# A four-layer graph network on one core: third norm merged with the attention projections, comparisons ahead of the scan, and an earlier clearing of a buffer

## The reference, cut to what matters

```python
x = _layernorm(x + _L0_gnn_ref(x, src, dst, edge_weight, W1, W2))     # two weighted sums over edges
x = _layernorm(x + _L1_gnn_ref(x, weight, w_comp, root, bias, ...))   # eight edge types
x = _layernorm(x + _L2_gnn_ref(x, W, b, src, dst, edge_weight))       # logmap, sum, relu, expmap
x = _layernorm(x + _L3_gnn_ref(x, edge_index, W, att_src, att_dst, bias))

# _L3_gnn_ref: attention with 8 heads of 16
xp = (x @ W).reshape(N, H, C)
a_src = einsum('nhc,hc->nh', xp, att_src);  a_dst = einsum('nhc,hc->nh', xp, att_dst)
e = leaky_relu(a_src[src] + a_dst[dst], 0.2)
m = segment_max(e, dst);  ex = exp(e - m[dst])
alpha = ex / (segment_sum(ex, dst)[dst] + 1e-16)
out = segment_sum(xp[src] * alpha[:, :, None], dst) + bias
```

## Time and profile before

| | us |
|---|---|
| median of 3 runs (lowest to highest) | 9468.76 (9463.22 to 9489.17) |
| profiled execution, its own time | 9472.64 |
| span of that execution | 9470.8 |

### The profile page before, as it was taken

The page is one execution under the profiler, slowest core; times in us unless marked ns, Lnnn a source line. Parts: engine busy times, 40 slices in busy tenths (PEclk is TensorE's granted clock), DMA queues, the critical chain, the costliest instruction groups (busy, mean ns, idle before and its releaser), DMA issues. The chain is left out here.

```text
span 9470.8 us, 285464 instructions
## 1 busy us (share of the span) xinstructions
PE 7599.4 (80%) x87223; PEld 6468.6 (68%) x87223; DVE 6462.5 (68%) x21922; ACT 2902.1 (31%) x8008; POOL 5787.9 (61%) x5766
## 2 busy tenths in 40 slices
PE   4887999998999996899999957999945666666662
PEld 4886999996999995466666646787834555555552
DVE  7997777775777776677777766676764555555556
ACT  3884222223222224322222242122241222222222
POOL 2663777773777772166666624666625777777771
PEclk7998999999999997999999978999976566655665
DMA  2002666664666665633333335555532222222223
GB/s 63 28 27 72 157 161 154 155 158 135 153 154 151 152 155 168 220 92 87 90 87 88 88 103 146 135 142 139 140 104 74 65 66 66 66 66 67 67 66 102
DMA packets 1057653, 1044.16 MB, mean 110 GB/s; under 512 B 171994, under 2 KB 957065, under 8 KB 1056897
## 3 DMA queue, kind: packets, MB, share of 16 engines
q1 hardware_dynamic: 869802, 654.88, 24.9%
q0 software_dynamic: 174080, 369.69, 16.8%
q10 hardware_dynamic: 13399, 16.26, 0.5%
HBM read 877.56 MB, written 169.10 MB: 111 GB/s over the span
## 5 line engine op out<-in xcount | busy, mean ns | idle before, releaser
L1048 DVE TENSOR_SCALAR state<-iota_row,state 128x128 f32<-128x128 f32 x5488 | 1444.4, 374 | 0.0
L1561 POOL DMA_INDIRECT state<-rel_table,state x1120 | 1065.2, 951 | 504.9 <-issue 323.1
L1107 PE MATMUL psum<-ring 128*128 128x128 bf16 x21276 | 1275.5, 221 | 58.1 <-DVE ring L1041 58.1
L1107 PEld LDWEIGHTS psum<-ring 128*128 128x128 bf16 x21276 | 1208.2, 99 | 109.8 <-issue 42.5
L1027 POOL DMA_INDIRECT ring<-rows,idx x980 | 957.5, 977 | 368.6 <-issue 327.7
L1027 POOL DMA_INDIRECT ring<-gcn_table,idx x980 | 957.5, 977 | 352.6 <-issue 324.8
L2612 POOL DMA_INDIRECT acc<-att_table,acc x896 | 935.0, 1043 | 273.1 <-issue 263.6
L1276 POOL DMA_INDIRECT state<-hyp_table,state x784 | 751.4, 958 | 419.5 <-issue 217.8
L2612 POOL DMA_INDIRECT ring<-att_table,acc x672 | 698.0, 1039 | 441.4 <-ACT acc L2654 245.4
L1122 PE MATMUL psum<-state 64*128 64x128 f32 x14112 | 958.7, 278 | 0.0
L1041 DVE TENSOR_SCALAR ring<-sel,iota_col 128x640 bf16<-128x640 bf16 (+1 forms) x1576 | 513.4, 369 | 600.3 <-PE psum L1107 581.6
(11 more groups left out here) (444 smaller groups left out, 14711.7 us busy)
## 6 DMA issues: line engine op xcount, KB each, us to landing
ring<-xparts SPq DMA_DIRECT2D x1332, 192.0 KB
ring<-srow SPq DMA_DIRECT2D x544, 128.0 KB
sel<-drow SPq DMA_DIRECT2D x394, 160.0 KB
sel<-drow SPq DMA_DIRECT2D x394, 128.0 KB
rel_table<-tout SPq DMA_DIRECT2D x98, 512.0 KB, 2.6
ring<-rows SPq DMA_DIRECT2D x56, 448.0 KB
xparts<-state SPq DMA_DIRECT2D x28, 672.0 KB, 3.6
rows<-acc SPq DMA_DIRECT2D x42, 448.0 KB
```

What stands on the lines that cost most here:

```text
L1048: ins = nc.vector.tensor_scalar(picks[u][:, j, :], iota_row[:, :], tabS[:, bass.ds(n * SJ + j, 1)], tabW[:, bass.ds(n * SJ + j, 1)], ALU.i ...
L1107: last = nc.tensor.matmul(rowsP[v][:, j * P:(j + 1) * P], reach[v][:, t, j * P:(j + 1) * P], xwin[u][:, t, i, :], start=(t + i == 0), stop ...
L1561: pool.indirect_dma_start(out=type_rows[j % RB][:, k, :], out_offset=None, in_=table, in_offset=bass.IndirectOffsetOnAxis(ap=type_idx[j % ...
```

## The change

- The third norm and the attention projections become one block, norm_into_attention. ACT scales the tiles into a stage instead of in place; the rows are stored and transposed from there. The transposes of even and odd blocks use two pairs of banks (0 and 1, 2 and 3). Each engine runs its steps with a lag to the others: DVE scales block b+2, copies the transposed rows of block b+1, adds and takes statistics of block b+3, and copies the product of block b.
- In the attention pass the selection is made by eight TENSOR_SCALAR comparisons of 128x128 instead of one TENSOR_TENSOR of 128x1024, and comes ahead of the scan; DVE waits for the scan's own end before it goes on.
- The row no_sums lies in rown and is filled in the setup; body is cleared in the sort, one DMA of 256 rows with each piece and one for the rest, and no longer in the first cell pass. An unused table, starts8, goes.

```diff
-        no_sums = sq[:, 0:ROW7]
+        no_sums = rown[:, 0:2, :].rearrange("p a t -> p (a t)")[:, 0:ROW7]
...
+                c(nc.vector.memset(no_sums[:, 0:ME], 0.0))
+                c(nc.vector.memset(no_sums[:, ME:ROW7], -BIG))
...
+                    def clear_rows(j):
+                        at = j * (PT * P)
+                        sp.dma_start(body[bass.ds(at, PT * P), :].rearrange("(t p) c -> p t c", p=P),
+                                     no_sums.unsqueeze(1).to_broadcast([P, PT, ROW7])
+                                     ).then_inc(sem("kept1"), 16)
...
                             keep(it * 2 + v)
                             load(it * 2 + (v + 2), v)
+                            clear_rows(it * 2 + v)
...
-                        if table is rows0:
-                            sp.dma_start(body[bass.ds(sg * SUMS, SUMS), :].rearrange("(t p) c -> p t c", p=P),
-                                         no_sums.unsqueeze(1).to_broadcast([P, SUMS // P, ROW7])
-                                         ).then_inc(sem("kept1"), 16)
...
+        def norm_into_attention():
...
+                @block.sync
+                    def step(it, u):
+                        load(it, u)
+                        keep(it, u)
+                        keep_table(it, u)
...
+                @block.scalar
+                            act.wait_ge(sem("var"), b + 1)
+                            nc.scalar.activation(sd[:, v, :], mv[:, v, :, 1], ACT.Sqrt, bias=eps_t[:, :]
+                                                 ).then_inc(sem("sdev"), 1)
+                            act.wait_ge(sem("scaled"), b + 1)
+                            act.wait_ge(sem("rowsT"), b + 1)
+                            act.wait_ge(sem(f"kept{v}"), turn * 16 + 16)
+                            act.sem_inc(sem("issued"), 1)
+                            for t in range(BT):
+                                last = nc.scalar.activation(stage[:, v, t * P:(t + 1) * P],
+                                                            acc[:, bass.ds(b * BW + t * P, P)], ACT.Identity,
+                                                            bias=shift[:, v, t:t + 1], scale=rstd[:, v, t:t + 1])
...
+                @block.tensor
+                    def transpose_block(it, u):
+                        b, v, _ = block_at(it, u, 2)
+                            pe.wait_ge(sem("normed"), b + 3)
+                            pe.wait_ge(sem("xTfree"), b + 1)
+                            for t in range(BT):
+                                last = nc.tensor.transpose(pblk(v)[:, t * P:(t + 1) * P],
+                                                           stage[:, v, t * P:(t + 1) * P], ident[:, :])
...
+                    def product(it, u):
+                        b, v, _ = block_at(it, u, 1)
+                            pe.wait_ge(sem("xTready"), b + 1)
+                            pe.wait_ge(sem("tB"), b + 1)
...
+                @block.vector
+                    def step(it, u):
+                        normalise(it, u)
+                        columns(it, u)
+                        sums_and_spread(it, u)
+                        table_rows(it, u)
...
                             nc.vector.tensor_tensor_scan(runmax, starts_T[w], sT, -BIG, ALU.add, ALU.max
                                                          ).then_inc(sem("runmax"), 1)
+                            dve.wait_ge(sem("runmax"), n + 1)
...
-                            nc.vector.tensor_tensor(
-                                sel_of[w], iota_row[:, :].unsqueeze(1).to_broadcast([P, K, P]),
-                                dstrel[:, bass.ds(n * K, K)].unsqueeze(2).to_broadcast([P, K, P]),
-                                ALU.is_equal).then_inc(sem("selected"), 1)
+                            for k in range(K):
+                                ins = nc.vector.tensor_scalar(sel_of[w][:, k, :], iota_row[:, :],
+                                                              dstrel[:, bass.ds(n * K + k, 1)], None,
+                                                              ALU.is_equal)
+                            ins.then_inc(sem("selected"), 1)
...
+                        select(i)
                         scan(i)
-                        select(i)
...
-                residual_norm("hyp", rows2, rows3 if layers > 3 else out)
+            if layers > 3:
+                norm_into_attention()
...
-            project("att")
             attention()
```

More of the change, by code:

```diff
@@ L698, in _ @@
                             load(it * 2 + (v + 2), v)
+                            clear_rows(it * 2 + v)
                     keep(PIECES - 3)
+                    for j in range(PIECES // 2 * 2 - 2, PIECES):
+                        clear_rows(j)
+                    sp.dma_start(body[PIECES * PT * P:NPAD, :].rearrange("(t p) c -> p t c", p=P),
+                                 no_sums.unsqueeze(1).to_broadcast([P, NPAD // P - PIECES * PT, ROW7])
+                                 ).then_inc(sem("kept1"), 16)
                     load(PIECES - 1, 0)
@@ L1010, in _ @@
                                 load(sg * GB + it * 4 + u, it * 4 + u, u)
-                    if table is rows0:
-                        sp.wait_ge(sem("kept1"), (SG + 1) * 16)
                     for u in range(4):
@@ L1051, in to_sources @@
                         ins.then_inc(sem("picked"), 1)
-                    if table is rows0:
-                        nc.vector.memset(no_sums[:, ME:ROW7], -BIG)
-                        nc.vector.memset(no_sums[:, 0:ME], 0.0).then_inc(sem("made"), 1)
                     nc.vector.memset(zeros_b, 0.0).then_inc(sem("sent"), 1)
@@ L2326, in project, with lagged, block_at, is_block @@
             fence()
+        def lagged(eng, step, lead):
+            for b in range(-lead, 0):
+                step(0, b)
+            with eng.Fori(0, NB // 2 - 3) as it:
+                step(it, 0)
+                step(it, 1)
+            for b in range(NB - 6, NB):
+                step(b // 2, b % 2)
+        def block_at(it, u, lead):
+            at = u + lead
+            return it * 2 + at, at % 2, it + at // 2
+        def is_block(b):
+            return not isinstance(b, int) or 0 <= b < NB
@@ L3088, in gnn_kernel @@
             row_factor("exp")
-            residual_norm("hyp", rows2, rows3 if layers > 3 else out)
+            if layers > 3:
+                norm_into_attention()
+            else:
+                residual_norm("hyp", rows2, out)
         if layers > 3:
-            project("att")
             attention()
```

114 lines of the change are left out of this document (108 added, 6 removed).

## The result

The changed kernel takes 9320.38 us (median of 4 runs, 9313.42 to 9322.51), the kernel before 9465.99 us beside it (4 runs, 9454.16 to 9489.17): a ratio of 0.9842, interval 0.9822 to 0.9862. TensorE's granted clock, averaged over the span, is nearly the same in both (0.855 after, 0.852 before of full speed).

The account below looks back on a forecast made before the run. POOL's back-to-back gathers were taken to bound the attention pass (1958 us plus 152.5 of stretching), DVE the norm. Gains 88 + 20 + 13 - 0.3 = 121 us off 9472.64 gave 9352, stated as 9350, range 9308 to 9408.

Parts of the forecast that it names:

- the likeliest case: Whole kernel: all three changes gain as summed, 9350 us, own range 9312 to 9392; chance 0.68.
- Part 1: Attention pass: eight scalar comparisons ahead of the scan gain 88 us, ends 38 and 138.
- part 2: Third norm and attention projections merged: 7.75 us a block, a gain of 20 us, ends 10 and 26.
- part 3: First cell pass: moving the clearing DMAs out gains 13 of its 16 us excess, ends 3 and 17.
- The limit of the attention pass: Attention pass: POOL's gathers follow one another without waiting for an index, 1958 us plus 152.5 us of stretching.
- The second rival: Attention pass: another limit keeps it from going below 10.77 us a group, total 9438; chance 0.06.
- The select's term: Attention pass: the old two-input comparison stretches gathers by 102 us, which the change removes.
- The scalar comparisons' term: Attention pass: the eight new comparisons cost the gathers 9 ns each, 14 us, ends 0 and 30.
- The products' term: Attention pass: the four products a group keep stretching gathers by 50 us, ends 0 and 100.
- The first rival: Attention pass: gathers fall into the products more often, 100 us instead of 50, total 9400; chance 0.13.
- The added wait: Attention pass: perhaps 0.2 us a group on DVE behind the scan, covered by its 4.5 us idle time.
- The third rival: Attention pass: the eight comparisons hold POOL as one block, 178 us instead of 102, total 9512; chance 0.09.

Follow-up runs that it names:

- e12: Changed kernel with the edges' weights written a second time by ACT, to PSUM, and read there by the products; 9291.96 us, ratio 0.9805.
- e2: Kernel before with only the merged norm and attention projections; 9454.49 us, ratio 0.9978.
- e3: Kernel before with only the earlier clearing (no_sums filled in the setup, body cleared in the sort); 9453.19 us, ratio 0.9983.
- e4: Changed kernel with one two-input 128x1024 comparison again, still ahead of the scan; 9431.78 us, ratio 0.9956.
- e5: Changed kernel with its eight scalar comparisons behind the scan, as in the old order; 9325.37 us, ratio 0.9837.
- e7: Changed kernel plus one unused 128x1024 scalar multiplication by a constant per group, ahead of the selection; 9366.58 us, ratio 0.9884.
- e11: Changed kernel plus one unused 128x1024 scalar comparison per group, its scalar read from SBUF, ahead of the selection; 9353.63 us, ratio 0.9870.
- e6: Changed kernel with the selection made by eight 128x128 comparisons of two SBUF inputs instead of eight scalar ones; 9492.73 us, ratio 1.0014.
- e8: Changed kernel plus one unused 128x608 maximum of two SBUF inputs per group, ahead of the selection; 9363.36 us, ratio 0.9876.
- e9: Changed kernel with the messages' products in eight instructions of 128x128 instead of four of 128x256; 9361.67 us, ratio 0.9879.
- e1: Kernel before with only the attention selection changed: eight scalar comparisons ahead of the scan, and the added wait; 9355.02 us, ratio 0.9878.
- e10: Changed kernel with the merged block's transposes all in one pair of PSUM banks (0 and 1); 9317.35 us, ratio 0.9832.

## Why the prediction was right, and where it was not

The forecast was 9350 us with 9308 to 9408; it came to 9320.38, inside the likeliest case's own range too. The sum was 121 us of gain, the profiled executions show 150. Part 1 gave 26 more than its term, part 2 6 and part 3 3, the second cell pass 1; setup (beyond its forecast 0.3), sort and unchanged stages take back some 7.

**The limit of the attention pass: right.** The prediction said that the gathers last 1568 times 1.249 us, 1958 us, plus the stretch. In all fourteen profiles they take 1956.6 to 1956.8 us plus the stretch, and POOL's gap stayed at 0.30 us. The second rival, another limit at 10.77 us a group, is false: between the same two points as the earlier trace rows a group takes 1995.60 / 196 = 10.18 us after, and 10.03 in e12.

**The select's term: right, its closeness partly luck.** 102 us were put down to it, measured are 87.7 + 8.9 = 96.6 in the trace it was read from, but 121 and 113 in e2 and e3, which run the same pass. All of it is gone after. The form and not the place did it (e4, e5).

**The scalar comparisons' term: somewhat too dear, and its reason in part wrong.** 14 us were given, 7.75 are measured. The prediction read from the cell passes that this form does not hold a gather. It does: e7 and e11 show scalar instructions of 0.69 and 0.74 us that hold one to their end. What makes the eight cheap is that each is short and that the gather gets in ahead of the next one, where e6's two-input comparisons did not let it in. After, 246 gathers met them and lost 32 ns each.

**The products' term: mis-sized, the largest error.** "The products stay at 50 us if they fall on the gathers as they do now", with ends of 0 and 100. Measured are 53.4 before and 29.0 after. The gathers in them went from 249 to 203 and the mean of one from 214 to 143 ns. This term of the sum was off: its price was taken over unchanged from one trace. Two things stand in the runs. First, 21.1 us of the stretch before are in 29 gathers that were kept beyond one product, by up to 860 ns, through a cast, the next product and a subtraction:
```profile
7866.80 0.42 DVE L2820 TENSOR_TENSOR acc<-acc 128x256 f32<-128x256 f32 x1
7866.82 1.80 POOL L2612 DMA_INDIRECT ring<-att_table,acc  x1 [0.30 <-issue]
7867.13 0.20 DVE L2741 CAST tout<-tout 128x72 bf16<-128x72 f32 x1
7867.24 0.42 DVE L2820 TENSOR_TENSOR acc<-acc 128x256 f32<-128x256 f32 x1
7867.57 0.23 DVE L2744 TENSOR_TENSOR tout<-tout 128x72 bf16<-128x72 f32 x1
```
After, the longest stretch at a product is 282 ns. But e2 and e3, with the pass of before, have none over 275 either and 40 and 37 us at the products, so these 21 us are that execution's and not the old code's, and the change took some 10 us from the products beside those two. Second, the phase moved, which the prediction had named but not sized: from the end of a group's eighth gather to ACT's first step on its rows (L2662 before, L2843 after) the median went from 2.8 to 4.7 us, with the DMA share from 0.26 to 0.28. Over the profiles it follows the pace of the gathers: 1.8 us in e6 at 11.08 us a group, 2.7 to 3.1 at 10.8 (before, e2, e3, e4), 4.1 to 4.3 at 10.4 (e7, e8, e9, e11), 4.7 at 10.2 and below (after, e1, e5, e10, e12). Why the rows come later when the gathers are issued faster stays open, and with it why fewer gathers start in a product. The first rival, more gathers in the products, is false by its sign.

**The added wait and DVE's 85 us: right.** DVE's idle time before the copy of the last maxima was forecast at about 4 us a group and is 3.4; no gather waits for it.

**The third rival, the eight as a block: false for this form, and what the other form does.** It forecast a stretch of 178 us at the comparisons for instructions that hold one after another, and 9512 us. In e6 they are that: 109.0 us of gathers that met the comparisons themselves and 81.4 in 42 gathers handed to them from a product, 190 together, and 9492.73 us.
The Trainium skill, in "SBUF — State Buffer", section "Who interferes with whom", has copies and scalar operations in two-port mode block GpSimd for the whole instruction, and infers that a two-input TENSOR_TENSOR leaves descriptor generation alone, though in general it has one with both inputs in SBUF contend with a GpSimd instruction that reads SBUF. By the first the long scalar instructions of e7 and e11 hold a gather; they do, by up to 507 and 483 ns, so the prediction was wrong to say that the trace had the page the other way round there. By the inference, e4 and e6 would show no stretch; they show 87.2 us at the comparison of e4 and 215.7 us in e6, and the measurement decides.

**Part 2: right, a little too small.** 7.75 us a block were forecast, 7.49 came: 14 x 0.26 = 3.6 us. The prediction added 0.15 to 0.3 for waits to 5.10 + 1.08 + 1.34 = 7.52, and they added nothing. TensorE's terms were too short and it did not matter: 0.93 and 1.98 us were read where the granted clock was 1.00. In the merged block it is 0.50 from 7066.64 to 7071.82, and there the products take 3.70 and the transposes 1.70:
```profile
7066.64 3.70 PE L2420 MATMUL psum<-Watt,sel 128*128 128x144 f32 x14 [3.10 <-DVE tout L2485]
7070.12 1.70 PE L2410 MATMUL psum<-ident,ring 128*128 128x128 f32 x7
```
Together that is 5.4 of 7.49 us. Ramp and tail were set at 7 us (7125.5 and 7 are 7132.5, not 7132.7): from the first addition, 7005.19, to the end of the last table copies, 7114.71, are 109.5 us, which leaves 4.6 beside 14 x 7.49 = 104.9. In the whole stage the gain is 25.9 us of 20 forecast. The run of e2 shows some 21 for 26.5 in its stage, since its attention pass came out 7.9 us longer than that of before with the same code (e3's came out 2.2 shorter). That the second pair of banks is needed for it was wrong (e10).

**Part 3: right.** 13 of 16 us were forecast, 16.2 came: the two cell passes are equal to 0.8 us, so all of their difference was the clearing and none the tables. The sort took 752.5 us instead of 749.5, but over all profiles it lies between 747.0 and 753.6, with the clears in it (747.0 in e9) and without (752.4 in e1, 752.8 in e2), so the 3 us are not theirs.

## What to carry to other kernels

When gathers issued by POOL set the pace, look at what DVE runs at each of their starts. A DVE instruction with both inputs in SBUF, or a long one with one input, can delay a gather to its own end, and some of those that follow keep it held. Two remedies are shown here. A comparison of two inputs was replaced by short scalar comparisons with the scalar in SBUF, which let the gather in ahead of each. And one input of the products was moved to PSUM: it cost DVE nothing here and took away 28 of 29 us. Do not split a two-input operation and keep its form: that made it worse twice (e6, e9). And take the price of such an overlap from more than one trace: with the same code the products' share was 53, 40 and 37 us.

## What the runs showed of the hardware

- A gather (DMA_INDIRECT, 944 ns undisturbed) that is held ends 0.82 us after the DVE instruction that let it go, for a two-input product (8008.59, 9.41), a comparison of 1.19 us and a scalar instruction of 0.69 us (7872.29, 7873.11) alike. Held by one instruction alone, it is stretched by what is left of that instruction 0.12 us after the gather's start.
- Whether an instruction holds a gather that starts close to its own start varies. Beside the products of after, the 26 gathers that started up to 0.04 us ahead of one were not stretched by it, and all that started 0.04 to 0.26 us behind its start were. At the comparison of 128x1024 before, which follows the scan, six gathers that started 0.04 us ahead of it were held to its end (1108 to 1113 ns) and four that started 0.07 to 0.16 us ahead were not; in e11 one that started 0.055 us behind the long instruction's start was not.
- Eight scalar comparisons of 128x128 without a pause, 1.66 us, stretch a gather by at most 124 ns (138 in e12); eight two-input ones, 1.70 us, by up to 1438 ns when it starts inside them and up to 2480 ns when it was handed to them from a product.
- A held gather was let in ahead of each scalar comparison with its scalar in SBUF and ahead of the scan with an input in PSUM, every time; ahead of a scalar multiplication by a constant never in 20 times (table above, places without a pause).
- A TENSOR_TENSOR of 128x256 takes 0.41 us with one input in PSUM and 0.42 with both in SBUF. The second held gathers by up to 282 ns by itself, the first by at most 38.
- In the merged block DVE is busy 6.6 of 7.49 us, whether the granted clock of TensorE is 0.73 or 0.50. Seven transposes take 0.93 us at a granted clock of 1.00 and 1.70 at 0.50, fourteen products 1.98 and 3.70.
